# The last mixture of experts: three of eight batches computed by dispatched 128-row expert tiles

## The chip, the core and the metric

The kernel runs on one core of a Trainium2 chip. The core has five engines with their own instruction streams: TensorE (PE, with its weight loads shown as PEld), VectorE (DVE), ScalarE (ACT), GpSimd (POOL) and SyncE (SP, which issues most DMAs). They meet only through semaphores. The metric is the device time of one execution in microseconds (us), lower is better.

## The reference, cut to what matters

Four layers are added to a residual `x` of 8 batches x 512 tokens x 128 channels: a delta-rule attention, a mixture of 8 experts, a gated linear attention with a small MLP behind it, and a last mixture of 16 experts, of which each token uses the 4 with the largest router probabilities. The change touches the last one:

```python
logits = hidden_states @ router_w + router_b
probs = jax.nn.softmax(logits, axis=-1)
topw, topi = jax.lax.top_k(probs, K)                 # E = 16, K = 4
topw = topw / jnp.sum(topw, axis=-1, keepdims=True)
combine = jnp.sum(one_hot(topi, E) * topw[..., None], axis=2)
def body(acc, expert):                               # once for each expert
    w1e, b1e, w2e, b2e, ce = expert                  # 128x256, 256, 256x128, 128
    hmid = jax.nn.gelu(x @ w1e + b1e, approximate=False)
    return (acc + (hmid @ w2e + b2e) * ce[:, None], None)
```

The reference computes all 16 experts for every token and multiplies 12 of them by zero.

## The kernel before, in words

The kernel does as the reference does. Its last stage walks over 8 batches x 16 experts, 128 units in all. A unit takes the 512 tokens of one batch through one expert. Numbers are split into two float16 halves ("high" and "low", the low one being the rounding error of the high one), and each product is three float16 matmuls: high x high, high x low, low x high (`PARTS`, line 395). For one unit:

- PE, `hidden1` (line 2357): for each half of the 256 hidden channels three matmuls of 512 columns, weights stationary, into one of PSUM banks 0 to 3.
- ACT (line 1185): two Gelus with the bias of the expert (line 1191) into `h_full`, then one copy to float16, `h_high` (line 1195, 128x1024).
- POOL (line 745): `h_low = h_full - h_high` (128x1024).
- PE, `outputs1` (line 2367): 4 token tiles x 6 matmuls of 128 columns into bank 4 or 5.
- DVE, `accumulate` (line 1851, the instruction at 1857): four 128x128 steps, `resid += coefficient * bank`.

`hidden1` runs three units ahead of `outputs1` (`AHEAD`, line 2355). The output bias of all 16 experts is added once a batch: the coefficients are transposed (`coefficients_transposed`) and multiplied with `mb2_hl`, and DVE adds the result (line 1896).

Between the units of batch b, each engine does a part of the "chain" of batch b+1, at fixed expert numbers: normalise, transpose, the MLP of the layer before (`hidden11`, Gelu, `outputs11`, also in float16 halves except for batch 0), add, normalise, transpose, split, router logits, the four largest, the weights. It all goes through PSUM bank 6. On PE and ACT seven batches run in a hardware loop (`Fori`), on DVE and POOL the code is unrolled; the last batch is written out on every engine. An operand whose address depends on the loop's variable has it worked out in PE's sequencer; the profile shows such work as FUSED_REGOPS and ALU_OP on the line of the matmul.

The order of work on each engine is written out by hand. SP writes a batch out when its last unit is added (line 545). PE's matmul helper is line 1909, its transposes are line 1916.

The first mixture, an earlier stage, already dispatches: POOL scatters rows of tokens to DRAM with indirect DMAs (line 655) and expert outputs back (line 672), and DVE combines them (line 1572).

Of the kernel before, what the change touches and what calls it, by code (L numbers as in the profile page):

```python
# [18 lines left out]
def build(nc, I, out):  # L19
    f32, f16, i32, u32 = mybir.dt.float32, mybir.dt.float16, mybir.dt.int32, mybir.dt.uint32  # L20
    ALU = mybir.AluOpType
# [6 lines left out]
    NT = T // 128  # L28
# [13 lines left out]
    with ctx:  # L42
# [13 lines left out]
        A6, A7 = (sb(f"A{n}", [128, B * T]) for n in range(6, 8))  # L56
# [11 lines left out]
        expand = sb("expand", [128, B, 128])  # L68
# [25 lines left out]
        mb2 = sb("mb2", [3 * E1, C])  # L94

# [16 lines left out]
        YROWS = TOP0 * TILES * 128  # L112
        disp = nc.dram_tensor("disp", (ROWS, RW), f32).ap()
        y_rows = nc.dram_tensor("y_rows", (YROWS, C), f32).ap()

# [6 lines left out]
        def at(n, k=0):  # L122
# [13 lines left out]
                    "gate_low", "yg1_ready", "z_added",   "mlp_added", "xn12", "split_low", "m0_low", "xdT", "x_low", "lg12_added", "lg_less", "z_stats", "hid11_low"],  # L136
# [4 lines left out]
        signals = {n: sem(n) for v in SIGNALS.values() for n in v}  # L141

        def S(name):
            return signals[name]
# [15 lines left out]
        s_eb2_mm = sem("eb2_spread")  # L160
# [8 lines left out]
        s_rn, s_wide, RN = s_var, s_std, len(GROUPS)  # L169

# [139 lines left out]
        hT11_hl = carve(8)[:, 512:1024].bitcast(f16).rearrange("p (s t) -> p s t", s=2)  # L310
        hid11_high = carve(2)[:, 512:1024].bitcast(f16).rearrange("p (i t) -> p i t", i=2)
        hid11_low = carve(3).bitcast(f16).rearrange("p (i t) -> p i t", i=2)[:, :, 512:1024]
        u1_hl = w_r1[:, 256:512].bitcast(f16).rearrange("p (s n) -> p s n", s=2)
        u2_hl = [v[:, :].bitcast(f16).rearrange("p (i c) -> p i c", i=2) for v in (w_v, w_o)]

# [21 lines left out]
        P7 = bank(7)  # L337
# [8 lines left out]
        g1s = carve(7)[0:16, 0:512]  # L346

# [62 lines left out]

        block = ctx.enter_context(nc.Block())
# [3 lines left out]
        def _(sp):  # L415
# [50 lines left out]
            for k in range(3):  # L466
                load(mb2[k * E1:(k + 1) * E1, :], I["L1_ffn_b2"])
            assert count == W_LOADS
# [60 lines left out]
            for b in range(B):  # L529
                c = bts(b, T)  # L530
                sp.wait_ge(S("kq_low"), at(b))
                for dst, half, src in ((k_stack, 0, (0, 1)), (q_stack, 1, (1, 0))):
                    for k in range(2):
# [6 lines left out]
                         I["L1_ffn_w2"].rearrange("e (i p) c -> p e i c", p=128)).then_inc(s_wm, 16)  # L540
            ov = out.rearrange("b (n p) c -> b p n c", p=128)
            for b in range(B):
                sp.wait_ge(S("m1_bias"), at(b))
                sp.wait_ge(S("m1_acc"), at(b * E1 + E1 - 1))
                sp.dma_start(ov[b], resid[:, b * NT:(b + 1) * NT, :]).then_inc(s_out, 16)
            sp.wait_ge(s_out, X_LAST + 16 * B)
# [3 lines left out]
        def _(pool):  # L550
# [14 lines left out]
            pool.memset(expand[:, :, :], 0.0)  # L565
# [14 lines left out]
            sel(out=expand[:, :, :].rearrange("p b (h i) -> p b h i", i=D),  # L580
                in_=expand[:, :, :].rearrange("p b (h i) -> p b h i", i=D),
                compare_op=ALU.not_equal, fill=1.0, base=0, pattern=[[-H, B], [-1, H], [0, D]], channel_multiplier=1)
# [60 lines left out]
            def scatter(b):  # L643
# [4 lines left out]
                for t in range(NT):  # L648
                    if t == NT // 2 and b + 1 < B:
                        pool.wait_ge(S("lg5_mm"), at(b + 1))  # L650
                    elif t == NT // 2:
                        pool.wait_ge(s_eb2_mm, 1)
# [25 lines left out]

            def make_z(b):
# [56 lines left out]
            for k in range(B - 2):  # L736
                low_weights(k)


            for b in range(B):  # L740
                for e in range(E1):
                    n = b * E1 + e
                    pool.wait_ge(S("m1_high"), at(n))
                    pool.wait_ge(S("m1_out_mm"), at(n, 4))
                    pool.tensor_tensor(h_low[n % 4], h_full[n % 2], h_high[n % 4], SUB).then_inc(S("m1_low"), 1)  # L745
# [1713 lines left out]
```

## Time and profile before

| what | us |
|---|---|
| device time, median of 3 runs | 923.57 (923.51 to 925.18) |
| profiled execution, first to last instruction | 921.2 |
| PE busy | 775.8 (84%) |
| DVE busy | 693.3 (75%) |
| POOL busy | 628.8 (68%) |
| ACT busy | 628.6 (68%) |

The span is one profiled execution; the profile gives it no time of its own beyond the span, which lies 2.4 us under the median of the runs. The last stage begins at about 538 us with the first `outputs1` and ends at 916.5 us with the last `accumulate`; the write of the last batch and the ending of the program follow.

### The profile page before, as it was taken

To read this page: it belongs to the slowest core of one execution; us is meant where nothing else is said; L and a number is where in the kernel's file an instruction comes from. 1 tells how busy PE (TensorE), PEld (TensorE's weight loads), DVE (VectorE), ACT (ScalarE), POOL (GpSimd) and SP (SyncE) were. 2 spreads that over 40 slices of the span, in tenths; PEclk is the share of its full clock that TensorE was granted. 3 is DMA by queue.
4 is the path that set the end of the run, shared out by engine and by line. 5 is a ranking of instruction groups with operands and counts; after the bars stand their busy time and mean duration, and the time that the engine had idled before them with its cause. 6 is when DMAs were issued, how large, how long until landed. Compare 5 with 4: busy or idle time off the path is not lost.

```text
span 921.2 us, 18395 instructions
## 1 busy us (share of the span) xinstructions
PE 775.8 (84%) x6152; PEld 470.1 (51%) x6152; DVE 693.3 (75%) x2078; ACT 628.6 (68%) x938; POOL 628.8 (68%) x414
## 2 busy tenths in 40 slices
PE   4965765568998789378778989999999999999997
PEld 1343221124453357223233756777677777677775
DVE  7769799994777578598899878766666666666664
ACT  3855233323455567259788988898888888889895
POOL 4008899730477727466888997686868686868695
PEclk9987889999999799769999999999999999999999
DMA  5999300007200030252600000000000000000000
GB/s 149 119 121 207 113 0 0 15 6 194 87 21 7 4 103 25 82 147 50 202 1 1 1 2 2 12 1 11 0 11 0 12 0 0 11 0 11 0 13 13
DMA packets 52792, 40.47 MB, mean 44 GB/s; under 512 B 6059, under 2 KB 44734, under 8 KB 52734
## 3 DMA queue, kind: packets, MB, share of 16 engines
q1 hardware_dynamic: 49662, 37.28, 18.5%
q0 software_dynamic: 3072, 2.51, 1.0%
q8 instruction: 24, 0.39, 0.2%
q14 instruction: 34, 0.28, 0.1%
HBM read 18.07 MB, written 14.88 MB: 36 GB/s over the span
## 4 chain that ended last, share of the span: by engine, by line
POOL 24%; PE 19%; issue 14%; DVE 14%; ACT 6%; DMA 1%; POOLq 0%; DVEq 0%; ACTq 0%; SPq 0%
POOL scratch L745 21%; PE PS L1909 17%; DVE scratch L1670 2%; DVE resid L1572 2%; DVE stats L1407 1%; DVE scratch L1678 1%; POOL resid L731 1%; PE PS L1916 1%; POOL disp L655 1%; ACT scratch L1195 1%; ACT scratch L1191 1%; DVE resid L1420 1%; DVE A L1432 1%; DVE scratch L1410 1%; ACT A L1126 1%
## 5 line engine op out<-in xcount | busy, mean ns | idle before, releaser
L745 POOL TENSOR_TENSOR scratch<-scratch 128x1024 f16<-128x1024 f32 x128 | 272.9, 2134 | 84.5 <-ACT scratch L1195 82.4
L1857 DVE SCALAR_TENSOR_TENSOR resid<-PS,coef,resid 128x128 f32<-128x128 f32 x512 | 144.0, 344 | 108.9 <-PE PS L1909 103.6
L1909 PEld LDWEIGHTS PS<-A,scratch 128*128 128x128 f16 x3456 | 203.4, 98 | 37.8 <-POOL scratch L745 4.8
L1909 PE MATMUL PS<-A,scratch 128*128 128x128 f16 x3456 | 217.1, 219 | 3.9 <-POOL scratch L745 1.6
L1909 PE MATMUL PS<-A 128*128 (+1 forms) x768 | 186.8, 379 | 0.8 <-DVE A L1701 0.2
L1191 ACT ACTIVATE scratch<-PS,cols 128x512 f32<-128x512 f32 x256 | 163.8, 683 | 25.8 <-PE PS L1909 18.9
L1195 ACT ACTIVATE scratch<-scratch 128x1024 f16<-128x1024 f32 x128 | 135.3, 1057 | 5.0
L1909 PE MATMUL PS<-scratch,ident 128*128 128x512 f32 x160 | 88.3, 673 | 52.9 <-DVE scratch L1373 52.9
L614 POOL TENSOR_TENSOR scratch<-A 128x1024 f32<-128x1024 f32 x32 | 76.0, 2383 | 73.8 <-DVE A L1342 56.5
L1909 PEld LDWEIGHTS PS<-A 128*128 128x128 f16 x768 | 70.7, 98 | 66.6 <-issue 0.6
L655 POOL DMA_INDIRECT disp<-A,scratch x64 | 62.9, 982 | 36.5 <-issue 30.2
L1909 PEld LDWEIGHTS PS<-scratch,ident 128*128 128x128 f32 x160 | 30.7, 209 | 100.2 <-DVE scratch L1373 78.1
L1364 DVE TENSOR_TENSOR_SCAN PS<-PS,scratch 128x512 f32<-128x512 f32 x64 | 74.9, 1215 | 1.9
L1909 PE MATMUL PS<-scratch,A 128*128 128x512 f16 (+1 forms) x216 | 52.8, 390 | 1.4 <-DVE scratch L1520 0.7
L672 POOL DMA_INDIRECT y_rows<-A x32 | 34.2, 1070 | 27.6 <-DVE A L1535 23.6
L1916 PE MATMUL PS<-ident,scratch 128*128 128x128 f32 x128 | 21.4, 294 | 33.4 <-ACT scratch L981 15.5
L694 POOL TENSOR_TENSOR scratch<-scratch,A 128x1024 f32<-128x1024 f32 x16 | 38.3, 2394 | 13.1 <-DVE scratch L1670 4.9
L1909 PE MATMUL PS<-scratch,w_r 128*8 128x512 f32 (+1 forms) x106 | 40.2, 509 | 5.9 <-DVE scratch L1753 3.0
L838 ACT ACTIVATE PS<-A 128x512 f32<-128x512 f32 x33 | 19.7, 599 | 35.8 <-DVE PS L1364 35.8
L683 POOL TENSOR_SCALAR A<-resid,scratch 128x128 f32<-128x128 f32 x32 | 31.3, 989 | 18.5 <-DVE scratch L1584 18.5
L838 ACT ACTIVATE PS<-scratch 128x512 f32<-128x512 f32 x31 | 18.6, 601 | 36.6 <-DVE PS L1364 35.5
L1670 DVE TENSOR_TENSOR_SCAN scratch<-PS,scratch 128x512 f32<-128x512 f32 x32 | 37.3, 1206 | 3.1 <-POOL scratch L694 1.2
(336 smaller groups left out, 1330.9 us busy)
## 6 DMA issues: line engine op xcount, KB each, us to landing
A<-A SPq DMA_DIRECT2D x22, 256.0 KB, 7.4
y_rows<-zeros SPq DMA_DIRECT2D x8, 512.0 KB, 6.0
A<-y_rows SPq DMA_DIRECT2D x14, 256.0 KB, 3.5
disp<-zeros SPq DMA_DIRECT2D x4, 528.0 KB, 21.1
resid<-in_L_attn_x SPq DMA_DIRECT2D x8, 256.0 KB, 4.0
A<-scratch SPq DMA_DIRECT2D x8, 256.0 KB, 6.6
A<-in_L_ffn_ew SPq DMA_DIRECT2D x1, 2048.0 KB, 12.3
A<-scratch SPq DMA_DIRECT2D x32, 64.0 KB, 2.0
```

What stands on the lines that cost most here:

```text
L614: pool.tensor_tensor(c_ring[n % 3], bkR[:, 2 * p:2 * p + 2, :], vR[:, i, :].unsqueeze(1).to_broadcast([128, 2, T]), MUL).then_inc(S("r0_c" ...
L655: pool.indirect_dma_start(out=disp[:, :], in_=rows5[RING_OF[b]][:, k, t, :], in_offset=None, out_offset=bass.IndirectOffsetOnAxis(ap=slot_ ...
L672: pool.indirect_dma_start(out=y_rows[:, :], in_=eo[:, ex * NT + t, :], in_offset=None, out_offset=bass.IndirectOffsetOnAxis(ap=xd[:, ex * ...
L694: pool.tensor_tensor(cbuf[n % 2], cs[n % 2], v1[:, bts(b, T)].unsqueeze(1).to_broadcast([128, 2, T]), MUL).then_inc(S("r_c"), 1)
L745: pool.tensor_tensor(h_low[n % 4], h_full[n % 2], h_high[n % 4], SUB).then_inc(S("m1_low"), 1)
L838: A_(bank(n % 2), kk_pair(a, m)[:, max(i, j) % 2, :], ACT.Identity, scale=-1.0, bias=1.0).then_inc(S("r0_decay"), 1)
L1191: A_(h_full[e % 2][:, h * T:(h + 1) * T], bank((e * HC1 + h) % 4), ACT.Gelu, scale=1.0 / SCALE, bias=cols[:, MB1 + e * HC1 + h:MB1 + e * H ...
L1195: A_(h_high[e % 4], h_full[e % 2], ACT.Copy).then_inc(S("m1_high"), 1)
L1364: V.tensor_tensor_scan(out=bank(2 + 2 * (n % 2) + u), data0=bank(u), data1=c_ring[n % 3][:, u, :], initial=0.0, op0=MUL, op1=ADD).then_inc ...
L1670: last = V.tensor_tensor_scan(out=state[:, j, :], data0=bank(2 + j), data1=cbuf[n % 2][:, j, :], initial=0.0, op0=MUL, op1=ADD)
L1857: last = STT(out=resid[:, g, :], in0=bank(4 + e % 2)[:, t * C:(t + 1) * C], scalar=coef[b % 2][:, t, e:e + 1], in1=resid[:, g, :], op0=MUL ...
L1909: return nc.tensor.matmul(o, l, r, start=start, stop=stop)
```

## The change

Five batches (`DENSE` = 0, 1, 3, 6, 7) are computed as before. Three (`SPARSE` = 2, 4, 5) are dispatched: every token's row is scattered to a region of its expert in DRAM, once for each of its 4 experts, and read back as tiles of 128 rows of one expert. Four tiles make a group, a unit of its own; there are always 16 groups, the most that 6144 rows in 16 experts can need. So 128 units become 80 + 16 = 96. Units 0 to 57 are dense, units 58 to 81 hold the 16 groups with a dense unit ahead of every second one, and units 82 to 95 are dense.

- Routing of a sparse batch: logits in float32 from `A3`; one-hots counted on PE (`count_rows`), places on DVE (`place_rows`), ids by POOL's iota; rows as two float16 halves (`high_rows` on ACT, `low_rows` on DVE), copied three times by SP; 16 indirect scatters by POOL. `list_tiles` on DVE (some 16 small steps, at unit 43) makes for each tile its expert's weight column and its first row; `list_transposed` brings the list to one partition, from where PE and SP load it into registers, four values at a time.
- A group: SP loads four tiles (4 DMAs with addresses from registers); PE transposes them (8 float16 transposes, five units ahead), ACT copies them (128x1024 float16); `hidden1` has for each half and tile one bias matmul (one-hot of the expert times `mb1_hl`) and three of 128 columns whose stationary weights come from a register's address; `outputs1` one bias matmul and six whose moving weights do; DVE evicts (`evict`) instead of accumulating; POOL scatters four tiles of outputs to `y12`.
- At the end SP reads `y12` back and `combine12` on DVE adds it with the weights: 48 steps of 128x128, placed behind the last three units.
- `h_low` moves from POOL to DVE in the units where POOL scatters (`LOW_BY_DVE`: the even units 26 to 54, 47 to 54, 57 to 85, and the one behind each start of a chain).
- The chains start at units -2, 6, 13, 20, 27, 31 and 44 and are longer (up to 21 units); even batches use bank 6 and odd ones bank 7. The MLP of every batch is float32 now. The loops on PE and ACT are unrolled.

The diff, cut to its core:

```diff
+        DENSE, SPARSE = (0, 1, 3, 6, 7), (2, 4, 5)
+        CHAIN_AT = (None, -2, 6, 13, 20, 27, 31, 44)
+        GT = 4
+        FIRST_DENSE, LAST_DENSE, COMBINE_BEHIND = 58, 8, 5
+        GROUPS12 = -(-((NS * T * TOP1 + E1 * 127) // 128) // GT)
+        for g in range(GROUPS12):
+            if g % 2 == 0 and len(left) > LAST_DENSE:
+                UNITS.append(left.pop(0))
+            UNITS.append(("group", g, 0))
+        AHEAD, TR_AHEAD, SCATTER_BEHIND = 3, 5, 3
+        XT_RING, YO_RING, XG_RING = 7, 4, 3
+        SCATTER_AT = [CHAIN_AT[b] + 20 for b in SPARSE]
+        for i in range(NS - 1):
+            for n in range(TOP1 * NT):
+                SCATTERS.setdefault(SCATTER_AT[i] + n // 2 * 2, []).append((i, n))
+        for n in range(TOP1 * NT):
+            SCATTERS.setdefault(SCATTER_AT[NS - 1] + n // TOP1, []).append((NS - 1, n))
+        LIST_AT = CHAIN_AT[SPARSE[-1]] + 18
...
+            for g in range(GROUPS12):                                  # SP
+                if g >= XT_RING:
+                    n = g - XT_RING
+                    sp.wait_ge(*since(s_yo[n % YO_RING], 16 * GT * (n // YO_RING + 1)))
+                first_row = registers(mybir.EngineType.SP, tile_list[:, 128 + GT * g:128 + GT * g + GT], NOBODY)
+                for t, r in enumerate(first_row):
+                    sp.dma_start(xt[g % XT_RING][:, t, :], disp12[bass.ds(r, 128), :]).then_inc(s_xt[g % XT_RING][0], 16)
...
+            for u in range(NU):                                        # POOL
+                if LOW_BY_POOL[u]:
+                    low_half(u)
...
+                for i, n in SCATTERS.get(u, ()):
+                    scatter_tokens(i, n)
+                if u >= SCATTER_BEHIND and UNITS[u - SCATTER_BEHIND][0] == "group":
+                    scatter_outputs(UNITS[u - SCATTER_BEHIND][1])
...
+            for u in range(NU):                                        # DVE
+                if u + 2 < NU and not LOW_BY_POOL[u + 2]:
+                    low_half(u + 2)
+                if kind == "dense":
+                    accumulate(u, i, e)
+                else:
+                    evict(u, i)
+                chain_steps(u)
+                n = u - NU + LAST_DENSE - COMBINE_BEHIND
+                if 0 <= n < NS:
+                    combine12(n)
+                if u == LIST_AT - 2:
+                    list_tiles()
...
+            def weight_columns(u):                                     # PE
+                for g in range(GROUPS12):
+                    if LIST_UNITS_AT[g] == u:
+                        weights_at[g] = registers(mybir.EngineType.PE, tile_list[:, GT * g:GT * g + GT], (E1 - 1) * HC1 * 128)
...
+                for h in range(HC1):                                   # hidden1 of a group
+                    pe.wait_ge(S("m1_hid"), at(2 * u + h, 4))
+                    for t, w in enumerate(weights_at[i]):
+                        out = tile(bank((2 * u + h) % 4), t)
+                        mm(out, mb1_hl[:, h * 128:h * 128 + 128], picked_expert(i, t), stop=False)
+                        for k, (sw, sx) in enumerate(PARTS):
+                            last = mm(out, w1_hl[:, sw, bass.ds(w + h * 128, 128)], tile(x, sx * GT + t), start=False,
+                                      stop=k == len(PARTS) - 1)
...
+                    if kind == "group":                                # outputs1 of a group, for each tile t
+                        mm(out, picked_expert(i, t), mb2_hl, stop=False)
+                        for h in range(HC1):
+                            for k, (sw, sh) in enumerate(PARTS):
+                                part = (h_high, h_low)[sh][u % 4][:, h * T + t * 128:h * T + t * 128 + 128]
+                                last = mm(out, part, w2_hl[:, sw, bass.ds(weights_at[i][t] + h * 128, 128)], start=False,
+                                          stop=k == len(PARTS) - 1 and h == HC1 - 1)
```

## Rows read from the trace of the kernel before

**Rows 1.** The page: tenths busy in 40 slices of the span, and the granted clock.
```profile
PE   4965765568998789378778989999999999999997
POOL 4008899730477727466888997686868686868695
PEclk9987889999999799769999999999999999999999
```

**Rows 2.** Busy time by stretch: from:to, length, then each engine's busy us (count), clock, DMA.
```profile
core 0: us, PE busy (x) PEld busy (x) DVE busy (x) ACT busy (x) POOL busy (x), PEclk, DMA share, GB/s
539.00:589.00 50.00, 45.23 (x509) 32.71 (x510) 37.49 (x174) 40.26 (x56) 37.27 (x21) 1.00 0.01 2
...
588.90:636.70 47.80, 47.44 (x543) 34.56 (x541) 32.95 (x131) 42.46 (x56) 36.54 (x19) 1.00 0.02 6
...
875.80:915.10 39.30, 39.30 (x475) 29.59 (x471) 21.67 (x79) 33.76 (x44) 33.01 (x16) 1.00 0.03 9
```

**Rows 3.** Timeline of PE in the last batch: start us, us, instructions in order.
```profile
878.50 1.46 PE L1909 MATMUL PS<-A 128*128 128x512 f16 x6
879.80 1.50 PE L1909 MATMUL PS<-A,scratch 128*128 128x128 f16 x24
881.14 1.46 PE L1909 MATMUL PS<-A 128*128 128x512 f16 x6
```

**Rows 4.** Waits between 589 and 876 us: who for whom, us in total, times, longest.
```profile
POOL scratch L745 <- ACT scratch L1195: 71.1, 73, 5.4
...
PEld PS L1909 <- POOL scratch L745: 2.7, 6, 0.5
```

**Rows 5.** Source line 1909 from 674.45 to 675.5 us: count, ns, first and last start.
```profile
L1909 PE MATMUL PS<-coef,A x12: 169/169/181, 675.2 to 675.5; 128*128 128x16 f16 x12
L1909 PEldq FUSED_REGOPS  x8: 46/46/65, 674.5 to 675.4; - x8
```

**Rows 6.** Timeline of PE: the float32 MLP of batch 0, and the float16 one of batch 1.
```profile
515.88 1.12 PE L1909 MATMUL PS<-scratch,u 128*128 128x512 f32 x2
516.84 1.05 PE L1909 MATMUL PS<-u_o,A 128*128 128x128 f32 x8
...
519.68 2.05 PE L1909 MATMUL PS<-u,scratch 128*128 128x128 f32 x16
521.57 0.28 PE L1909 MATMUL PS<-ident,scratch 128*128 128x128 f32 x1
...
597.27 0.81 PE L1909 MATMUL PS<-scratch,w_r 128*128 128x512 f16 x3
597.92 1.46 PE L1909 MATMUL PS<-A 128*128 x6
```

**Rows 7.** The page's groups: busy us, mean ns of one, idle before and its releaser.
```profile
L745 POOL TENSOR_TENSOR scratch<-scratch 128x1024 f16<-128x1024 f32 x128 | 272.9, 2134 | 84.5 <-ACT scratch L1195 82.4
...
L1191 ACT ACTIVATE scratch<-PS,cols 128x512 f32<-128x512 f32 x256 | 163.8, 683 | 25.8 <-PE PS L1909 18.9
L1195 ACT ACTIVATE scratch<-scratch 128x1024 f16<-128x1024 f32 x128 | 135.3, 1057 | 5.0
```

**Rows 8.** Timeline of DVE: one unit's accumulate, a combine, and a two-input step.
```profile
655.07 1.13 DVE L1857 SCALAR_TENSOR_TENSOR resid<-PS,coef,resid 128x128 f32<-128x128 f32 x4 [2.52 <-PE PS L1909]
...
393.14 2.31 DVE L1572 SCALAR_TENSOR_TENSOR resid<-A,scratch,resid 128x128 f32<-128x128 f32 x8
...
339.72 1.21 DVE L1501 SCALAR_TENSOR_TENSOR A<-A 128x1024 f16<-128x1024 f32 x1
```

**Rows 9.** Timeline of POOL: scatters, idle before each in brackets.
```profile
245.68 0.97 POOL L655 DMA_INDIRECT disp<-A,scratch  x1 [0.31 <-issue]
246.95 0.97 POOL L655 DMA_INDIRECT disp<-A,scratch  x1 [0.30 <-issue]
...
340.04 1.74 POOL L672 DMA_INDIRECT y_rows<-A  x1 [0.30 <-DVE A L1535]
```

**Rows 10.** DMA issues by line: count, KB each, median us to landing.
```profile
disp<-A,scratch POOLq DMA_INDIRECT x64, 2.1
A<-disp SPq DMA_DIRECT2D x2, 264.0 KB, 3.1
```

**Rows 11.** The chain that ended last, its last pieces: start us, us, what.
```profile
867.09 46.33 PE PS L1909 x540
...
915.41 1.12 DVE resid L1857 x4
```

More of the change, by code:

```diff
@@ L409, in build, with registers @@
         fetched = [v[:, :].rearrange("p (n c) -> p n c", c=C) for v in (A6, A7)]
+        def registers(engine, values, most):
+            return nc.values_load_multi_w_load_instructions(
+                values, engines=[engine], min_val=0, max_val=most,
+                skip_runtime_bounds_check_because="made on VectorE from counts that add up to the rows")[1]
         block = ctx.enter_context(nc.Block())
@@ new lines, in _ @@
+            copy_rows(0)
+            written_out(DENSE[0], LAST_UNIT[0])
+            copy_rows(1)
+            written_out(DENSE[1], LAST_UNIT[1])
+            copy_rows(2)
+            sp.wait_ge(*after("tiles_listed", 0))
+            for k in range(E1 // 4):
+                first_free = registers(mybir.EngineType.SP, tail_row[:, 4 * k:4 * k + 4], NOBODY - 128)
+                for r in first_free:
+                    sp.dma_start(disp12[bass.ds(r, 128), :], zeros[:, :]).then_inc(s_tail[0], 16)
@@ L546, in _ @@
+            written_out(DENSE[4], LAST_UNIT[4])
+            for i in range(NS):
+                sp.wait_ge(*after("y_combined", i))
+                sp.dma_start(ov[SPARSE[i]], resid[:, bts(SPARSE[i], NT), :]).then_inc(s_out, 16)
             sp.wait_ge(s_out, X_LAST + 16 * B)
@@ L737, in _ @@
                 low_weights(k)
[L740 to L745, printed above, removed]
[L746 to L749 removed]
+            add_up(1)
@@ L1903, in _ @@
+            for i in range(max(0, LAST_DENSE - COMBINE_BEHIND), NS):
+                combine12(i)
             dve.drain().then_inc(stage_done, 1)
@@ L2418, in _, with list_transposed @@
+            def list_transposed():
+                pe.wait_ge(*after("tile_values", 0))
+                chain_bank_read(0)
+                for k in range(2):
+                    mm(bank(6)[0:1, 128 * k:128 * k + 128], tile_values[:, k:k + 1], ident[:, :])
+                last = mm(bank(6)[0:3 * E1, 256:384], tile_expert, ident[:, :])
+                last.then_inc(S("tiles_mm"), 1)
+                read_by[0] = after("tiles_listed", 0)
+            hidden1(0)
             project1(5)
-            hidden1(0, 1)
+            hidden1(1)
```

706 lines of the change are left out of this document (484 added, 222 removed).

## The prediction

> **What bounds the kernel now.** I read the page's slices first, to find the stage that the change touches. From slice 24 on (538 us) PE stands at nine tenths to the end and its granted clock is at full speed, while POOL lies at six to nine [rows 1]. Then busy time by stretch. The loop's batches repeat at 47.8 us with PE busy for 47.4 of it, ACT 42.5, POOL 36.5 and DVE 33.0. The last batch has no chain beside it and takes 39.3 us, all of it PE [rows 2]. The waits agree: POOL waits for ACT (71.1 us in 287) and costs nothing by it, since PE waits for POOL for 2.7 us [rows 4]. So the stage is PE's, and a unit costs what its matmuls cost. The timeline of the last batch gives that: six matmuls of 512 columns from 878.50 to 879.80, 24 of 128 from 879.80 to 881.14, so 1.30 + 1.34 = 2.64 us, or 0.056 us for one of 128 columns [rows 3]. Sixteen units are 42.2 us. The remaining 5.6 us of a batch are its chain.
>
> The end: PE's run ends at 913.4, a last accumulate at 916.5, and the write-out follows [rows 11].
>
> **The change part by part.** I count against the profiled execution (921.2 us) and carry the difference to the median, 2.4 us higher.
>
> *Removed.* 128 - 80 = 48 dense units on a full PE: 48 x 2.64 = -126.5 us.
>
> *Groups on PE's array.* A group has 32 + 28 = 60 matmuls of 128 columns and 8 transposes, 68 x 0.056 = 3.8 us.
>
> *Groups on PE's sequencer.* Weight addresses come from registers. The nearest thing in the trace is the router's logits in the loop: 12 short matmuls with 8 different addresses have 8 FUSED_REGOPS, each shown as 46 ns, but starting from 674.5 to 675.4, so 0.9 / 7 = 0.13 us apart [rows 5]. Two of the three products share an address, so I take two such steps for each tile and half of each layer: 4 x 2 x 2 x 2 = 32, or 4.1 us a group. If each matmul makes its own it is 48, or 6.2. Loading four registers is in no row. From below it is one step of 0.13; from above a DMA's 2.1 us to landing [rows 10]; nearest is four steps, 0.5. Explicit waits: 0.4. Together 5.0 us a group, of which much runs ahead of the array while it waits. The Trainium skill (DMA: Bandwidth & Descriptors, "Latency and other measured facts") gives a register load a floor of about 600 ns. No row here shows one; by that figure the sum would grow by 16 x 0.1 us.
>
> *Groups on the other engines.* I work in pairs, as the order has it: one dense unit and two groups. Array: 2.64 + 2 x 3.8 = 10.2. Sequencer: 10.0. ACT: two Gelus, a copy and a copy of the gathered rows at the same 1.06, so 2 x 3.5 + 2.4 = 9.4 [rows 7]. DVE: an accumulate (1.13), two evictions of 0.7 and three low halves of 1.21, so 6.2 [rows 8]. POOL: eight scatters, 1.27 us from start to start [rows 9], 10.2. But a scatter also took 1.74 instead of 0.97 us when it started under DVE's 1.21 us step with both inputs in SBUF [rows 8, 9]. The low half is such a step. I take half of that 0.77 (most of its neighbours lost less), 3 x 0.4, so POOL needs 11.4. Five figures between 9 and 11.5 leave no slack; I take the largest, 11.5 us a pair. Bounds: 10.2 and 17.6 (rival 1). Eight pairs hold 8 of the 80 dense units, so the groups add 8 x 11.5 - 8 x 2.64 = +70.9.
>
> That last slowing is a rule of the Trainium skill as well (GPSIMD Engine Reference, "Key points"): GpSimd shares SBUF interfaces with VectorE and contends with VectorE instructions that have two SBUF inputs. By the rule in full, every scatter pays; without it the pair is 10.2 and the sum 10 us lower.
>
> *Chain on PE.* The MLP goes to float32: one 512-column product is 516.84 - 515.88 = 0.96 us against 597.92 - 597.27 = 0.65, twice; the second layer 521.57 - 519.68 = 1.89 against 24 x 0.056 = 1.35 [rows 6]. That is +1.16, less 0.3 of waits for DVE's splits, which go: +0.8 a batch, seven times 5.6. A sparse batch loses coefficients and output bias (0.9 in all) and gets 8 small count matmuls: -0.8 three times. The list: +0.4. Sum +3.6.
>
> *Units 20 to 43.* Chains of batches 3 to 6 overlap here. DVE had 33.0 - 16 x 1.13 = 14.9 us of chain a batch, of which 3.5 were the float16 splits that go, so 11.4 stay. DVE: 24 x 1.13 + 11 low halves x 1.21 + 3.4 chains x 11.4 = 79. PE: 24 x 2.64 + 17 = 80. ACT comes to 76. In before PE had a quarter of DVE's time as cover; here it has none, and each engine waits for the others in a fixed order. I take +6, between 0 and 12.
>
> *Units 43 to 58: the wait for the first tiles.* From unit 44 to 54 POOL has nothing but scatters. The last sparse batch's places are ready some 3.6 us after PE's unit 43 (accumulate, then five small DVE steps). Then 24 scatters (16 of batch 5 and 8 of batch 4 left over by the order) take 24 x 1.27 = 30.5, plus 9 low halves x 0.4. Add 2.1 to landing [rows 10], 0.5 for SP's registers and 3.1 for a load of 264 KB [rows 10]: 43.4. PE wants the first tiles behind unit 54, after 11 x 2.64 + 5.7 of chains = 34.7. In order as it is, it stands: +9. Behind PE's wait stand `hidden1` of all later units, so nothing fills it. DVE, with 12 accumulates, 10 low halves, a list of some 16 steps and the chains of 6 and 7, comes to about 44 itself, so taking the scatters away alone would not give the 9 back. Bounds: 0 (POOL runs ahead further) and 24 (rival 3).
>
> *Behind the groups.* If POOL is a few us late with the last outputs, the low half of unit 86 is late: +2. SP's reading back of 3 MB lies beside 12 dense units (32 us) and is hidden; uncovered it would be some 15.
>
> *The tail.* 48 combine steps run at 2.31 / 8 = 0.29 [rows 8], 13.9, and three accumulates, 3.4, all behind PE's unit 93: 17.3. Before, from unit 125 to the last accumulate 5.1 us pass (PE 3.6, DVE 1.5). +12.
>
> *Moved at no cost.* Gathering copies by SP (256 KB) lie between units 12 and 16 of a chain, under PE; the zero rows behind the regions lie under the scatters; three more small loads and a POOL mask less at the start are under the first stage's work. Unrolled code on PE and ACT: the last batch was straight code already and PE had no gap in it [rows 2].
>
> **Sum:** -126.5 + 70.9 + 3.6 + 6 + 9 + 2 + 12 = -23.0, so 898.2 for the profile and 901 for the median.
>
> **The rivals.** *1, slower: the sequencer sets the pace.* 48 address steps (6.2), a load at 2.1 and waits 0.5 make 8.8 a group and 17.6 a pair; 8 x 6.1 = +49, so 950. It takes the whole gain from 14.4 us a pair on. For it: address steps are the only rows that are longer apart than a matmul of 128 columns. Against it: 8 for 12 in the trace, not 12 [rows 5].
>
> *2, faster: no friction.* POOL is not slowed, the pair is 10.2 (-10), and the stands of 6, 9 and 2 vanish in the slack: -27, so 874. For it: the three-units-ahead order absorbed ACT's table loads before. Against it: the wait behind unit 54 is arithmetic of 24 scatters.
>
> *3, slower: GpSimd's scatters at 1.74 throughout.* 2.04 us each: the first tiles come after 58.3 instead of 43.4 (+14), the ring of four output buffers holds PE back by 7, and unit 86 waits for the last of 131 us of scatters, +22. So 944. It cancels the gain from about 1.7 us a scatter. Against it: only two of 32 took that long.
>
> That there are fewer or more groups than 16 is ruled out by the code.
>
> **How the numbers follow.** Forecast 0.50, rival 1 0.15, rival 2 0.20, rival 3 0.10, something unseen and slow 0.05. Under 0.2% (1.8 us) a measurement can't tell from no change. Of the forecast's half, 0.45 falls faster (its own range is 886 to 918), with rival 2 and the milder parts of 1 and 3 that makes 0.71; within 0.2% 0.05; slower 0.24. The range 876 to 936 leaves out the full rivals 1 and 3 and the last part of 2.
>
> **What would show it.** Right: 80 dense units at 2.64 us; pairs of about 11.5 between units 58 and 81; PE idle before the first group's transposes, released by a DMA; scatters between 0.97 and 1.74; PE done some 15 us before DVE. Wrong: FUSED_REGOPS on PE at 48 a group, or pairs over 14 us; a second stand of PE, behind DVE's low halves, in units 20 to 43 above 12 us; tiles that wait for POOL throughout.

## The result: 989.2 us, slower, where 901 was forecast

The kernel after takes 989.23 us (median of 3, 989.0 to 989.61) against 923.57: the ratio is 1.0704, with a 95% interval of 1.0685 to 1.0724. The sign was wrong, and the time lies outside the range.

The profiled execution has a span of 987.9 us against 921.2. I cut both at the start of the last matmul of a unit's second layer ("unit 0 at" is that time for unit 0). The forecast of a stretch is made of the prediction's own terms. Before needs 376.4 us from its first to its last unit, of which 332.3 are the units' own matmuls and 44.1 the chains.

| stretch | forecast, us | measured, us |
|---|---|---|
| start to unit 0 | 538.6 (as before) | 558.2 |
| unit 0 to 57, the chains and the first tiles | 57 x 2.64 + 44.1 + 3.6 + 6 + 9 = 213 | 261.7 |
| unit 57 to 81, the sixteen groups | 8 x 11.5 = 92 | 117.7 |
| unit 81 to the last (95) | 33.2 + 2 = 35 | 33.2 |
| the last unit to the end | 6.2 + 12 = 18 | 17.1 |

Three rows carry the 90 us of the miss: the first 19.6, the second 49, the third 26. The last two are as forecast.

The page after, in the same slices as [rows 1]:

```profile
PE   4876555689997892787787769879686969999993
POOL 3019898602777374668897636546466852565682
PEclk9977899899997997899997889979899979999997
```

From slice 24 on, where before PE stood at nine tenths to the end, there are now sixes and sevens among the nines, and the granted clock is down at 0.7 to 0.9 in many slices. So PE waits. Busy time by stretch, as [rows 2] (from:to, length, busy us and count, clock, DMA share, GB/s):

```profile
700.00:720.00 20.00, 16.11 (x140) 11.12 (x140) 13.82 (x54) 14.45 (x19) 5.81 (x5) 0.83 0.22 64
840.00:860.00 20.00, 20.00 (x217) 13.57 (x216) 8.02 (x14) 11.82 (x16) 11.85 (x10) 1.00 0.27 73
937.60:970.80 33.20, 33.20 (x405) 25.19 (x403) 17.95 (x57) 25.27 (x33) 28.01 (x17) 1.00 0.37 97
```

The two losses differ in kind. Around 710 us PE has idle time. Around 850, in the groups, it has none: no engine is waited for, and the array itself takes 15.3 us a pair instead of the forecast 10.2.

Whom PE waits for from 530 us on (us in total, times, longest). Of the 21.5 us in the first row, 9.7 lie ahead of unit 0 and 11.8 behind it:

```profile
PE PS L2230 <- DVE scratch L1949: 21.5, 7, 5.8
PE PS L2223 <- DVE resid L2115: 12.4, 9, 3.3
PE PS L2766 <- DMA A<-disp: 7.3, 1, 7.3
PE PS L2223 <- ACT scratch L1332: 3.9, 1, 3.9
```

Before, from unit 0 on, the largest such row was 4.1 us, for VectorE's splits (L1753), which the change removes; the 2.7 us for POOL in [rows 4] are waits of the weight loads (PEld).

L1949 is the normalisation of a chain. The timeline of VectorE shows what became of it, after and then before (a second profile of before; start, us, four steps in a row):

```profile
514.74 4.32 DVE L1949 SCALAR_TENSOR_TENSOR scratch<-A,scratch 128x128 f32<-128x128 f32 x4
531.09 4.43 DVE L1949 SCALAR_TENSOR_TENSOR scratch<-resid,scratch 128x128 f32<-128x128 f32 x4
```

```profile
514.12 1.12 DVE L1734 SCALAR_TENSOR_TENSOR scratch<-A,scratch,PS 128x128 f32<-128x128 f32 x4
525.77 1.12 DVE L1734 SCALAR_TENSOR_TENSOR scratch<-resid,scratch,PS 128x128 f32<-128x128 f32 x4
```

The same four steps on the same sizes take four times as long. The one difference stands in the operands: `PS` is gone. The diff has that line, and the prediction never speaks of it: `P7`, the scratch of every small routing and normalising step, moved from PSUM bank 7 into SBUF, since the chains now use two banks. GpSimd meanwhile ran, after and then before, and was as busy in both:

```profile
511.38 7.53 POOL L853 TENSOR_TENSOR A<-A 128x512 f32<-128x512 f32 x6
...
530.73 5.81 POOL L873 TENSOR_TENSOR A<-A 128x512 f16<-128x512 f32 x5 [0.89 <-ACT A L1307]
```

```profile
510.76 7.41 POOL L705 TENSOR_TENSOR A<-A 128x512 f32<-128x512 f32 x6
...
525.40 6.74 POOL L725 TENSOR_TENSOR A<-A 128x512 f16<-128x512 f32 x6 [0.18 <-ACT A L1126]
```

And a group's first layer, PE's timeline after:

```profile
839.98 0.23 PE L2223 MATMUL PS<-nr,mb_hl 48*128 48x128 f16 x1
840.14 0.34 PE L2223 MATMUL PS<-A 128*128 128x128 f16 x3
840.41 0.23 PE L2223 MATMUL PS<-nr,mb_hl 48*128 48x128 f16 x1
840.57 0.34 PE L2223 MATMUL PS<-A 128*128 128x128 f16 x3
```

Four matmuls, one bias product over 48 rows and three over 128, repeat every 0.43 us; at the 0.056 us of [rows 3] they would take 0.22. From a 48-row product to the next start 0.16 us pass, and as much back from the last 128-row one.

That gave three theories. **A**: the scratch in SBUF, whose short steps stand behind GpSimd's long ones, costs the start and the chains. **B**: the change of rows, 48 to 128 and back, costs the groups. **The rival** of both: the float32 MLP, the overlap of the chains, and PE's sequencer (rival 1) in the groups.

### The profile page after: what moved, and what is told of

It reads as the page before. It is cut to its first block and busy times, and to the rows that moved or that the text cites. A ratio compares the mean times of both kernels' runs of the same rounds, so it can differ in the third digit from the quotient of the medians.

```text
span 987.9 us, 17581 instructions
## 1 busy us (share of the span) xinstructions
PE 778.8 (79%) x5724; PEld 462.6 (47%) x5724; DVE 742.8 (75%) x1998; ACT 570.0 (58%) x856; POOL 583.6 (59%) x445
## 3 DMA queue, kind: packets, MB, share of 16 engines
q1 hardware_dynamic: 72510, 48.32, 22.3%
## 5 line engine op out<-in xcount | busy, mean ns | idle before, releaser
L2223 PE MATMUL PS<-A,scratch 128*128 128x128 f16 (+1 forms) x2688 | 181.4, 222 | 14.7 <-DVE resid L2115 12.4
L2223 PEld LDWEIGHTS PS<-A,scratch 128*128 128x128 f16 x2688 | 160.6, 99 | 43.0 <-issue 19.1
L2223 PE MATMUL PS<-A 128*128 128x512 f16 (+1 forms) x864 | 167.7, 319 | 0.1
L891 POOL TENSOR_TENSOR scratch<-scratch 128x1024 f16<-128x1024 f32 x45 | 97.8, 2177 | 88.6 <-ACT scratch L1395 87.9
L2115 DVE SCALAR_TENSOR_TENSOR resid<-PS,coef,resid 128x128 f32<-128x128 f32 x320 | 89.8, 343 | 70.4 <-PE PS L2223 64.4
L1388 ACT ACTIVATE scratch<-PS,cols 128x512 f32<-128x512 f32 x160 | 101.5, 684 | 68.3 <-DVE scratch L2129 33.0
L761 POOL TENSOR_TENSOR scratch<-A 128x1024 f32<-128x1024 f32 x32 | 75.9, 2379 | 77.3 <-DVE A L1554 59.3
L2223 PEld LDWEIGHTS PS<-A 128*128 128x128 f16 (+1 forms) x864 | 68.4, 100 | 60.1 <-issue 15.1
L802 POOL DMA_INDIRECT disp<-A,scratch x64 | 62.9, 982 | 36.4 <-issue 30.0
L2230 PE MATMUL PS<-ident,scratch 128*128 128x128 f32 x128 | 24.4, 323 | 58.8 <-DVE scratch L1949 24.5
L905 POOL DMA_INDIRECT disp<-A,scratch x48 | 58.2, 1212 | 20.5 <-issue 12.0
L2129 DVE TENSOR_TENSOR scratch<-scratch 128x1024 f16<-128x1024 f32 x51 | 62.1, 1218 | 0.3
L913 POOL DMA_INDIRECT y<-A x32 | 36.6, 1145 | 22.2 <-DVE A L2123 13.5
```

The lines of the kernel that those rows point to most:

```text
L761: pool.tensor_tensor(c_ring[n % 3], bkR[:, 2 * p:2 * p + 2, :], vR[:, i, :].unsqueeze(1).to_broadcast([128, 2, T]), MUL).then_inc(S("r0_c" ...
L802: pool.indirect_dma_start(out=disp[:, :], in_=rows5[RING_OF[b]][:, k, t, :], in_offset=None, out_offset=bass.IndirectOffsetOnAxis(ap=slot_ ...
L891: pool.tensor_tensor(h_low[u % 4], h_full[u % 2], h_high[u % 4], SUB).then_inc(S("m1_low"), 1)
L905: pool.indirect_dma_start(out=disp12[:, :], in_=rows12[i][:, k, t, :], in_offset=None, out_offset=bass.IndirectOffsetOnAxis(ap=slot12[i][: ...
L913: pool.indirect_dma_start(out=y12[:, :], in_=yo[g % YO_RING][:, t, :], in_offset=None, out_offset=bass.IndirectOffsetOnAxis(ap=xt[g % XT_R ...
L1388: A_(h_full[u % 2][:, h * T:(h + 1) * T], bank((2 * u + h) % 4), ACT.Gelu, scale=1.0 / SCALE, bias=cols[:, MB1 + e * HC1 + h:MB1 + e * HC1 ...
```

## The experiments

The runs were made in five groups, each beside the kernel before. Its median there was 924 us once and 946 to 951 four times, with unchanged code, so ratios are compared, and stretches between units where both kernels have the same condition. What is known of the second condition, which the expectations call "late code", comes at the end (theory C).

**Scratch in SBUF, in the kernel before**

```
-        P7 = bank(7)
+        P7 = carve(8)[:, 0:512]
```

> The kernel before with one line of the change: the chain's small scratch (P7) in SBUF instead of a PSUM bank. Theory A (small VectorE steps with both inputs in SBUF stand behind GpSimd's long two-input steps; this is the larger part of the 19.6 us that the kernel after has lost before unit 0): 8 to 25 us slower than before, unit 0's last matmul 8 to 19 us later than 538.6, normalised steps of 3 us and more. Rival (the 19.6 us come from the float32 MLP, the new order or the added loads): within 2 us of before, unit 0 within 2 us.

Measured: 1066.8 us beside 948.4, ratio 1.124 (1.121 to 1.128). The one line costs 118 us, far above the expected 25: I had looked at the part before unit 0 alone, but eight chains pay. From first to last unit it is 486.0 us instead of 376.4, 110 of the 118; the 9 that are left must lie before unit 0, where 8 to 19 were expected. A batch loses time in two places: a unit there takes 10.9 and 7.1 us instead of 2.6, and the next after the longer one loses another 1.2. The steps (count, busy us, mean ns), in a later run of the same kernel and then in before:

```profile
L1728 DVE TENSOR_TENSOR scratch<-scratch 128x4 f32<-128x4 f32 x21 | 16.3, 777 | 0.7
L1725 DVE TENSOR_SCALAR scratch<-scratch 128x4 f32<-128x4 f32 x7 | 11.0, 1573 | 0.0
```

```profile
L1728 DVE TENSOR_TENSOR PS<-PS,scratch 128x4 f32<-128x4 f32 x21 | 3.6, 170 | 0.7
L1725 DVE TENSOR_SCALAR PS<-scratch 128x4 f32<-128x4 f32 x7 | 1.1, 153 | 0.0
```

A step over four numbers goes from 0.15 to 1.57 us in the mean. It is not its work: it waits for GpSimd's step to end. Steps of VectorE in the first of the two runs, and GpSimd's in the same stretch:

```profile
648.70 1.43 DVE L1808 TENSOR_TENSOR scratch<-scratch 128x64 f32<-128x64 f32 x1
650.16 1.19 DVE L1809 TENSOR_TENSOR scratch<-scratch 128x64 f32<-128x64 f32 x1
...
652.68 2.11 DVE L1813 CAST coef<-scratch 128x64 f16<-128x64 f32 x1
```

```profile
647.91 2.14 POOL L745 TENSOR_TENSOR scratch<-scratch 128x1024 f16<-128x1024 f32 x1 [0.22 <-ACT scratch L1195]
650.01 1.26 POOL L731 TENSOR_TENSOR resid<-resid,A 128x512 f32<-128x512 f32 x1
...
652.57 4.25 POOL L745 TENSOR_TENSOR scratch<-scratch 128x1024 f16<-128x1024 f32 x2
```

VectorE's steps end at 650.13, 651.35 and 654.79 us, each within 0.1 us of the end of a step of GpSimd (650.05, 651.27, and the first of the two from 652.57). In before the same three take 0.21 to 0.23 us beside a GpSimd that is as busy. Not each step pays: the one on line 1729 of the same form kept its 0.16 us. Once more, in another group:

> The kernel before with the chain's scratch in SBUF, once more. Theory A: 105 to 120 us slower than before on any chip (its units lose 7.0 and 10.8 us twice a batch, whatever the chip). If late code had a part in it: under 100.

Ratio 1.1246 (1.1226 to 1.1266), 117 us: theory A holds again. Before stood at 946 us beside it, so both runs were made in the second condition.

**Bias products over 128 rows, in the kernel after** (operands padded with zeros; 48 of 128 rows carry the biases)

```
-        mb1_hl = sb("mb1_hl", [3 * E1, HC1 * 128], f16)
+        mb1_hl = sb("mb1_hl", [128, HC1 * 128], f16)
...
-            return tile_picks[:, GT * g + t:GT * g + t + 1].to_broadcast([3 * E1, 128])
+            return tile_picks[:, GT * g + t:GT * g + t + 1].to_broadcast([128, 128])
```

> The kernel after with both bias products of the groups over 128 rows instead of 48 (operands padded with zeros; same number of matmuls, addresses and columns). Theory B (each change between 128 and 48 stationary rows costs the array some 0.2 us, 12 times a group, 2.5 us): groups from unit 57 to 81 fall from 117.7 to about 85 to 95 us, the whole by 20 to 33. Rival 1 of the prediction in another dress (PE's sequencer or its queue sets 6 us a group whatever the rows): 117.7 falls by 5 at most.

Measured: ratio 1.079 (1.075 to 1.083). Undisturbed pairs take 3.1 + 4.0 + 4.5 = 11.6 us instead of 15.3, as theory B has it, but the stretch of the groups was 122.5 us, far from the expected 85 to 95: in the disturbed pairs single units take 6 to 13 us, with many short stands of PE (16.1 us in 36, the longest 1.1) that its rows put down to issue, time in which it waits for nothing that the profile shows. The pattern fits B. Against the kernel after in the same condition (ratio 1.099, under theory C) the total is 19 us faster, just under the expected 20 to 33.

**Combines earlier, in the kernel after**

```
-        FIRST_DENSE, LAST_DENSE, COMBINE_BEHIND = 58, 8, 5
+        FIRST_DENSE, LAST_DENSE, COMBINE_BEHIND = 58, 8, 0
```

> The kernel after with the three combines of the sparse batches put behind units 88, 89 and 90 instead of behind unit 93 and the last. Tail as in the prediction's sum (VectorE's 48 combine steps lie behind the last matmul only by their place): 17.1 us from the last matmul to the end fall to 6 to 8, the whole by 7 to 11. Rival (the rows read back land late, VectorE stands before the combine and the accumulates and with them PE wait): 0 to 5 us slower.

Ratio 1.104 (1.100 to 1.108), not faster than the kernel after in this condition (1.099), though 7 to 11 us were expected. From the last unit to the end it is 6.9 us instead of 17.1, as expected, but PE stood longer: unit 91 came 11.3 us behind its forerunner and unit 93 8.6. VectorE did not wait for the rows; the combine itself was long. In this kernel, and in the kernel after:

```profile
1007.22 11.63 DVE L2144 SCALAR_TENSOR_TENSOR resid<-A,scratch,resid 128x128 f32<-128x128 f32 x16
```

```profile
974.88 4.65 DVE L2144 SCALAR_TENSOR_TENSOR resid<-A,scratch,resid 128x128 f32<-128x128 f32 x16
```

Beside GpSimd's low halves 16 steps with two SBUF inputs take 11.6 us, without them 4.7. This looks like theory A once more, at another line; a later run settles it.

**Normalisation with one tensor input, in the kernel after**

```
-    STT(out=dst, in0=src, scalar=mean, in1=r_P.to_broadcast([128, C]), op0=SUB, op1=MUL)
+    TS(dst, src, mean, r_P, SUB, MUL)
```

> The kernel after with the normalisation written as a step with one tensor input (mean and inverse deviation as per-partition scalars) instead of two tensor inputs in SBUF; scratch stays in SBUF. Theory A (two SBUF inputs are what is stretched from 1.1 to 4.4 us): unit 0 comes 5 to 8 us earlier, the waits of 5.8, 5.5 and 4.3 us of PE for the normalised rows shrink to 1 to 2, the whole 12 to 22 us faster. Rival (VectorE is stretched whatever its inputs, or these steps are only the last of a chain that is late anyway): 0 to 4 us faster.

Ratio 1.092 (1.089 to 1.095), some 7 us faster than the kernel after in this condition, not 12 to 22. From unit 0 to 43 it is only 3.3 us faster than the two kernels beside it that have the same code there (191.6 against 194.9 us), and the waits, again from 530 us on, stay:

```profile
PE PS L2229 <- DVE scratch L1949: 21.6, 8, 5.7
```

So my form of theory A fell: it isn't the number of inputs. `TENSOR_SCALAR` and `CAST` steps with one input were stretched to 2.1 us too. What they share is that input and output both lie in SBUF. Reductions, reciprocals and batch statistics between the same buffers kept the times that they have in before (0.15 to 0.28 us for the short ones). The Trainium skill (SBUF — State Buffer, "Who interferes with whom") has just this list: two SBUF inputs, or a copy, cast or tensor_scalar in a two-port mode, take the port pair that VectorE shares with GpSimd; and its section "SBUF: two separate sides" says that whoever issues first keeps it for the whole instruction. The traces agree, with 2.1 us for a step of 0.17. The prediction used this rule one way only, for scatters that stand behind VectorE.

**Scratch back in PSUM, in the kernel after** (bank 7 for `P7`; logits and exponentials stay in SBUF; the odd chains get bank 3, the hidden layer three banks)

```
-        P7 = carve(8)[:, 0:512]
+        P7 = bank(7)
-            return bank(6 + c % 2)
+            return bank(6 if c % 2 == 0 else 3)
...
-                        pe.wait_ge(S("m1_hid"), at(2 * u + h, 4))
+                        pe.wait_ge(S("m1_hid"), at(2 * u + h, 3))
-                            last = mm(bank((2 * u + h) % 4), w1_hl[:, sw, w],
+                            last = mm(bank((2 * u + h) % 3), w1_hl[:, sw, w],
```

> The kernel after with the chain's small scratch back in PSUM bank 7 (logits and exponentials, which ScalarE reads, stay in SBUF); the odd batches' chain gets bank 3 and the hidden layer runs in three banks instead of four. Theory A as the first runs sharpened it (VectorE steps that have only SBUF operands wait for GpSimd's running two-input step of 2.1 us; one PSUM operand takes them out of that): unit 0 at least 12 us earlier, PE's 21.5 us of waits for normalised rows under 6, units 0 to 57 at 215 to 235 us instead of 262, the whole 35 to 60 us faster than the kernel after. Rival (three hidden banks cost PE its lead, or the stand is of the overlapped chains themselves): under 15 us faster.

**And with the bias products over 128 rows**

> Both repairs: scratch in PSUM as in the run beside it, and the groups' bias products over 128 rows. Theories A and B together: the groups' stretch from 118 to about 90 us where code comes in time, so 25 us below the run with the scratch alone, and 60 to 85 below the kernel after; on the first chip's terms 905 to 925, within 2% of before. Rival (the array is not what the pairs wait for once ScalarE and GpSimd are as late as PE): under 10 us below the run with the scratch alone.

Beside them the kernels after and before, unchanged:

> The kernel after unchanged, on the chip of the runs beside it. Theory C (on some chips PE's code comes late while GpSimd's scatters run, seen as idle time put down to issue; the unrolled loop of the kernel after is exposed to it, the loop of before is not): on a chip where the kernel before takes 948, the kernel after takes 1035 to 1050 (ratio 1.09 to 1.105), and its units 43 to 58 stand 15 us longer than on the first chip. Without theory C: the first ratio, 1.070, on every chip.

> The kernel before unchanged, for its trace on the same chip as the runs beside it. Theory C: from unit 0 to the last it keeps 376 us (538.6 to 915.0) on any chip, and whatever is slower lies ahead of unit 0. Without it: the loop is as much slower as the rest.

| run | us | ratio, 95% | unit 0 at | 0 to 57 | 57 to 81 | 81 to 95 | to the end |
|---|---|---|---|---|---|---|---|
| before | 924.3 | | 539.6 | | | | |
| after | 987.8 | 1.068 (1.065 to 1.070) | 556.7 | 261.2 | 117.7 | 33.2 | 17.1 |
| scratch in PSUM | 947.6 | 1.025 (1.024 to 1.027) | 546.1 | 232.7 | 117.7 | 33.5 | 17.1 |
| both | 925.3 | 1.0016 (1.0007 to 1.0026) | 547.2 | 228.8 | 90.6 | 38.8 | 17.1 |

The scratch is worth 40.3 us, inside the expected 35 to 60, and in the two stretches where it was looked for: 10.6 us before unit 0 (at least 12 were expected) and 28.5 behind it. PE's waits for normalised rows fell from 21.5 to 9.0 us, not under 6. The rows are worth 22.3, and 27.1 in their own stretch. The first group of a pair in the run with both:

```profile
815.32 0.22 PE L2228 MATMUL PS<-nr,mb_hl 128*128 128x128 f16 x1
815.38 0.33 PE L2228 MATMUL PS<-A 128*128 128x128 f16 x3
815.54 0.22 PE L2228 MATMUL PS<-nr,mb_hl 128*128 128x128 f16 x1
815.60 0.33 PE L2228 MATMUL PS<-A 128*128 128x128 f16 x3
```

0.22 us for the same four matmuls, though these have more rows. But 16 groups with 12 such products at 0.21 us would be 40 us, not 27. The second group of the pair, in the same run:

```profile
819.21 0.22 PE L2228 MATMUL PS<-nr,mb_hl 128*128 128x128 f16 x1
819.27 0.51 PE L2228 MATMUL PS<-A 128*128 128x128 f16 x3
819.61 0.22 PE L2228 MATMUL PS<-nr,mb_hl 128*128 128x128 f16 x1
819.66 0.35 PE L2228 MATMUL PS<-A 128*128 128x128 f16 x3
819.85 0.22 PE L2228 MATMUL PS<-nr,mb_hl 128*128 128x128 f16 x1
```

```profile
L2228 PEldq FUSED_REGOPS  x27: 42/46/46, 818.7 to 822.3; - x27
```

Its fours start 0.24 to 0.40 us apart, and each four needs two address steps of PE's sequencer. These start 0.12 us apart for most of the pair (32 of them are 3.9 us), so in the second group they seem no longer to run ahead of the array. That fits the difference; no run tested it. Five us of the gain are given back behind unit 81: PE now comes to unit 86 before GpSimd is through with the last scatters, and its low half is late. The total, 925.3, stands at the upper end of the expected 905 to 925.

**The float32 MLP, in the kernel before** (in every batch instead of batch 0 alone; VectorE's splits go)

```
-                first = isinstance(c, int) and c == 0
+                first = True
-                            hid11_split(b + 1, 0)
```

> The kernel before with the chain's small MLP in float32 in every batch, as the change has it, instead of three float16 products; nothing else. By the prediction's term PE pays 1.16 us a batch and saves 0.3 of waits: +5.6 us over seven batches (0.6%), 928 to 931. Rival (VectorE's splits, 3.5 us a batch, were on the chain that PE waits for): 0 to 4 us faster. Another (a float32 product of 512 columns costs more than the one measured at 0.96 once PE is warm or cold): over 10 us slower.

953.1 us beside 950.6, ratio 1.0019 (1.0002 to 1.0036). From first to last unit it is 376.5 us against 376.4: neither 5.6 dearer nor cheaper. The rival "float32 MLP" is out, and the prediction's +5.6 for it was too much. PE's waits for VectorE's splits, 4.1 us in the whole loop of before, are gone, more than the 0.3 a batch that the prediction took off; why nothing of the rest shows was not followed up. Unit 0 came at 570.3 us here, against 538.6 in the first profile of before.

**The last 14 units, and the order at unit 0** (both repairs in all; low halves behind the groups by VectorE, combines behind units 88 or 91; then unit 0's second products ahead of batch 1's transposes)

```
-        LOW_BY_DVE |= set(range(UNIT_OF_GROUP[0] - 1, UNIT_OF_GROUP[-1] + 5))
+        LOW_BY_DVE |= set(range(UNIT_OF_GROUP[0] - 1, NU))
-        FIRST_DENSE, LAST_DENSE, COMBINE_BEHIND = 58, 8, 5
+        FIRST_DENSE, LAST_DENSE, COMBINE_BEHIND = 58, 8, 0    (3 in the second)
```

```
+            outputs1(0)
             transpose11(1)
```

> The kernel with both repairs (scratch in PSUM, bias products over 128 rows), and in it two more moves: all low halves behind the groups by VectorE instead of GpSimd, and the combines behind units 88 to 90. Theory A says why the early combines alone cost time (16 steps took 11.6 us beside GpSimd's low halves and 4.7 behind them): with GpSimd idle they take 4.7 each, the stand of 5.3 us behind unit 86 goes, VectorE has 33 + 14 us of work from unit 81 on and sets the end: 55.8 us from unit 81 to the end become 49 to 52, the whole 4 to 7 us faster than the kernel with both repairs, 917 to 921. Rival (the combines are long by themselves when they read freshly landed rows, or wait for them): not faster.

> As the run before it, with the combines behind units 91 to 93. VectorE has some slack from unit 82 to 91 that stays unused: 1 to 3 us slower than with the combines behind units 88 to 90, still 2 to 5 faster than the kernel with both repairs alone. If the rows read back land after unit 88's time, it is the faster of the two.

> The first of these runs, and PE's second products of unit 0 put ahead of the transposes of batch 1's normalised rows instead of behind them. Theory D (the kernel with both repairs comes 7.6 us later to unit 0 than the kernel before, because PE stands 3.8 us for these rows with the unit queued behind them, and 1.2 us in which its clock has fallen): unit 0 at 541 to 543 instead of 547.2, the whole 2 to 5 us faster. Rival (the rows are needed as soon anyway: the chain of batch 1 only stands later): within 1 us.

All in the second condition: ratios 1.054, 1.052 and 1.055. With GpSimd idle the combine is back at its short form, though the place is the early one:

```profile
967.52 4.65 DVE L2149 SCALAR_TENSOR_TENSOR resid<-A,scratch,resid 128x128 f32<-128x128 f32 x16
```

So theory A's reading of the long combine is right, and the rival (rows that have just landed) is out. But from unit 81 to the end the runs took 59.3, 56.9 and 52.8 us, where 49 to 52 was expected. In the third unit 0 came at 563.3 instead of 573.1, unit 1 then 8.3 us behind it, and at unit 20 3.2 us were left. Twice more with the combines behind 91, without and with the order at unit 0:

> Both repairs, low halves behind the groups by VectorE, combines behind units 91 to 93, once more. Where code comes in time: from unit 81 to the end 49 to 52 us instead of 55.8, the whole 917 to 920 beside 924 for the kernel before (ratio 0.992 to 0.996). With late code, as in the run before: ratio 1.05.

> As the run beside it, and the second products of unit 0 ahead of batch 1's transposes. Theory D: 2 to 4 us faster than the run beside it, since unit 20 came 3.2 us earlier of the 10 that unit 0 gained. Rival: the chain of batch 1 takes it back by unit 43, within 1 us.

Ratios 1.046 (1.042 to 1.050) and 1.041 (1.039 to 1.043). Unit 0 comes 6.6 us earlier, unit 20 0.6. A last pair on one chip:

> Both repairs, low halves behind the groups by VectorE, combines behind units 91 to 93, second products of unit 0 first. Where code comes in time: 914 to 920 beside 924 for before (ratio 0.989 to 0.996), 5 to 10 us below the run beside it. With late code: ratio 1.04, 5 to 10 us below the run beside it.

> Both repairs alone, once more, beside the run with the two moves. Where code comes in time: 925 (ratio 1.002) as measured. With late code: ratio 1.045 to 1.055.

1.043 (1.040 to 1.045) with the moves, 1.042 (1.038 to 1.046) without. Unit 0 is 5.7 us earlier and unit 20 1.1 later. From unit 81 to the end it is 56.4 against 52.9: PE's 35.8 become 46.7 and the tail's 17.1 become 9.8. VectorE now has an accumulate, a low half and the combines, 14 x 2.34 + 13.9 = 47 us in 33 us of PE's work, and sets the pace itself. Neither move brought the 5 to 10 us that were expected of the last run, and theory D (the stand ahead of unit 0 costs its length) fell: the chain of batch 1 takes it back. In the pair before, the medians differ by 5 us (991.3 and 986.1), but the two profiles by only 0.6. In the first condition, in which the groups are fast, the moves were never run.

**Theory C: the condition of the run**

> The kernel after unchanged. Theory C (late code is a matter of the chip): ratio 1.065 to 1.072 where the kernel before takes about 924, and 1.09 to 1.105 where it takes about 950, with stands of PE put down to issue between units 43 and 58.

1041.1 us beside 946.3, ratio 1.099 (1.096 to 1.102), against 1.068 and 1.070. What differs shows in the run with both repairs, once beside a before of 924 and once of 946. PE's waits from unit 43 to the last, first the one and then the other:

```profile
PE PS L2771 <- DMA A<-disp: 4.6, 1, 4.6
PE PS L2228 <- ACT scratch L1390: 3.9, 1, 3.9
```

```profile
PE PS L2228 <- issue: 32.8, 58, 1.9
PE PS L2228 <- ACT scratch L1390: 3.6, 2, 3.0
```

```profile
757.30 0.27 PE L2228 MATMUL PS<-A,scratch 128*128 128x128 f16 x2 [0.34 <-issue]
758.75 0.27 PE L2228 MATMUL PS<-A,scratch 128*128 128x128 f16 x2 [1.18 <-issue]
760.17 0.22 PE L2228 MATMUL PS<-A,scratch 128*128 128x128 f16 x1 [1.15 <-issue]
```

In the second condition PE gets one or two matmuls and then stands for 0.3 to 1.2 us, waiting for no semaphore, while GpSimd issues a scatter every 1.27 us. Units 43 to 57 take 75.6 us instead of 58.8 and the groups 123.6 instead of 90.6; units 0 to 43, where PE's rows name issue for 0.2 us, take the same 170 in both. A third part, 20.6 us of the 67, lies ahead of unit 0, in the stages before the last mixture, and what the kernel before loses seems to lie there altogether: with the float32 MLP its loop took 376.5 us in the second condition too. Late code (instructions that reach PE after their time) fits the stands, since the groups and the chains are straight code after and a loop before, but that was only argued; units 0 to 43 are straight code as well and lost nothing. Half of the theory is refuted: I had it as a matter of the chip, and the last pair ran on the very chip that had shown 924. What sets the condition, and what PE stands for in it, stay open.

## Why the prediction was wrong

*What bounds before* held: PE from unit 0 on; an undisturbed dense unit is 2.64 us after as before, and the 48 removed units are gone.

*The step that failed first is one that isn't there.* "Moved at no cost" lists the copies, the zero rows and the loads, and leaves out `P7`, so the move of the scratch from PSUM to SBUF stands in the sum at nothing. By the repair it is worth 39 to 40 us, more than the whole margin of the forecast (22.6 us): VectorE's short steps wait for GpSimd's, and PE for the chain. Its price could not have been read from a single row of before. But that an elementwise step with all operands in SBUF gets in GpSimd's way was in the prediction, from VectorE's side: [rows 8, 9]. The chain's steps are short and GpSimd's are 2.13 us long [rows 7], so here it is mostly VectorE that stands.

*"Groups on PE's array, 68 x 0.056 = 3.8 us"* is the mis-sized term. It counted 12 products over 48 rows as if they were like the others. They cost 0.21 us more each where nothing else holds the array up. By the repair they are worth 27.1 us, 1.7 a group: a pair takes 15.3 us, and 11.7 with all rows at 128. That the sixteen groups then take 90.6 us where 92 was forecast is luck in part. The 11.5 us of the forecast were GpSimd's; in the repaired run PE is busy for the whole 91 us and GpSimd for 65, with some 15 more between its scatters, and a pair on PE, which was to need 10.2, needs 11.7.

*Rival 1* named nearly the price (pairs of 17.6) but not the cause. A group has the forecast 32 address steps on PE's sequencer, 0.12 us apart (0.13 was forecast), and the same 32 are there with 128 rows, where a pair takes 11.7. The rival's 48 steps are out; that the 32 hold up the second group of a repaired pair is likely, as shown above, and not tested. The load of four registers (TENSOR_LOAD) took 0.33 us in the median on PE, under the 0.5 of the sum. Rival 3 is out: the token scatters took 1.21 us in the mean, 0.24 over the 0.97 of [rows 9], where I had allowed 0.4 for three in eight.

*Chain on PE +3.6*: the 5.6 in it for float32 measured nothing; its other terms were not measured. *Units 20 to 43, +6* (0 to 12): with the scratch in PSUM they take 93.1 us, of which 60.7 are matmuls of the units; a chain costs 44.1 / 7 = 6.3 us in before, so 21 for the 3.4 of them here, and 11 remain, at the upper bound. *The first tiles, +9*: PE stood 7.3 us on a DMA behind unit 54. *Behind the groups +2*: nothing while the groups were slow, 5.4 us once they were fast. *The tail, +12*: 10.9.

*A smaller omission*: batch 1's transposes stand ahead of unit 0's second products, so unit 0 comes 7.6 us later even with both repairs. With the order changed it comes 5.7 to 9.8 us earlier, but by unit 20 at most 3.2 us are left.

Of the 24 us between the repaired kernel (922.4 in the profile) and the sum (898.2), 8.6 lie before unit 0, 16 between unit 0 and 57, and 3 behind unit 81, less 1.4 in the groups (the forecasts of the stretches are rounded, and add up to 1 to 2 us less than the sum). What makes the 16 was not tested beyond this.

## What to carry to other kernels

Read the diff for where operands live, not only for what is computed: a buffer that moves from PSUM to SBUF can make elementwise VectorE steps wait until GpSimd's running step ends, and the price is then set by the length of that step (here up to 2.1 us for a step of 0.17, and 0.8 and 1.6 us in the mean for two that take 0.17 and 0.15). Keep the rows of stationary and moving operands the same within a run of short matmuls: here padding with zeros cost nothing, and the change did. And look twice before putting a combine with two SBUF inputs beside a GpSimd that works (11.6 us here against 4.7), or before replacing GpSimd by VectorE without adding up what VectorE then has.

## What was unexpected in the hardware

- Each excursion from 128 to 48 stationary rows cost 0.21 us for 16-bit matmuls of 128 columns: 0.43 us for four, against 0.22 with all at 128 rows.
- Reductions, reciprocals and batch statistics of VectorE, SBUF to SBUF, were not stretched beside GpSimd; tensor_tensor, scalar_tensor_tensor, tensor_scalar and cast were, up to 2.1 us each.
- The same kernel before took 924 us in one group and 946 to 951 in four others, one chip having shown both. The kernel with the groups and both repairs lost 7% in the second condition (925 to 990), the kernel before 2.4%. The cause is open.
- PE's sequencer started its address steps 0.12 us apart without a break for most of a pair of groups, though the profile shows each as 0.046 us.
- A float32 MLP in place of the one in float16 halves, with VectorE's splits gone, changed nothing in the loop (376.5 against 376.4 us).
